# Where the last node's edges are counted: from the graph stage into the recall stage

## The reference

```python
sim = jnp.einsum('bihd,bjhd->bhij', q, k)
sim = jnp.where(causal, sim, neg)
attn = jax.nn.softmax(sim, axis=-1)
out = jnp.einsum('bhij,bjhd->bhid', attn, v)
return out.transpose(0, 2, 1, 3).reshape(b, n, HEADS * DIM) @ Wo
```

```python
src = jnp.concatenate([edge_index[0], loops])
dst = jnp.concatenate([edge_index[1], loops])
e = jax.nn.leaky_relu(a_src[src] + a_dst[dst], negative_slope=0.2)
e_max = jax.ops.segment_max(e, dst, num_segments=M)
ee = jnp.exp(e - e_max[dst])
denom = jax.ops.segment_sum(ee, dst, num_segments=M)
alpha = ee / (denom[dst] + 1e-16)
msg = h[src] * alpha[:, :, None]
agg = jax.ops.segment_sum(msg, dst, num_segments=M)...
```

## Time and profile before

| | |
|---|---|
| median of 3 runs | 5757.28 us (5738.8, 5757.28, 5758.62) |
| the profiled execution | 5745.75 us, its span 5744.1 us |
| mean granted clock of TensorE | 0.846 of full speed |
| TensorE busy | 4668.1 us, 81% |
| VectorE busy | 3530.2 us, 61% |
| ScalarE busy | 2180.4 us, 38% |
| GpSimd busy | 948.0 us, 17% |

### The profile page before, as it was taken

One profiled execution on the slowest core, in us unless ns is written; L12 is line 12 of the kernel. 1 busy time (PEld: TensorE's weight loads), 2 busy tenths in 40 slices (PEclk: granted clock), 3 DMA queues, 4 the chain that ended last, 5 costly groups with the idle time before them and its releaser, 6 DMA issues. The chain is left out here.

```text
span 5744.1 us, 71347 instructions
## 1 busy us (share of the span) xinstructions
PE 4668.1 (81%) x24568; PEld 2826.2 (49%) x24568; DVE 3530.2 (61%) x8762; ACT 2180.4 (38%) x3699; POOL 948.0 (17%) x1055
## 2 busy tenths in 40 slices
PE   7884999999999999999988888884149999963334
PEld 3451444444444444445544444442149988962222
DVE  7547777777777777675525555543125577567655
ACT  1342444444444444444434444442014433420001
POOL 0122111111111111110000000001730000006861
PEclk9555999999999999999978788785579999975556
DMA  1004446555546456655434011001000000000110
GB/s 66 8 3 73 124 131 131 120 131 129 138 112 150 117 129 135 125 132 136 116 115 114 23 34 34 23 1 34 8 7 11 11 15 6 7 9 7 19 13 12
DMA packets 324633, 389.07 MB, mean 68 GB/s; under 512 B 119857, under 2 KB 274749, under 8 KB 323492
## 3 DMA queue, kind: packets, MB, share of 16 engines
q1 hardware_dynamic: 233848, 185.45, 15.8%
q0 software_dynamic: 58368, 172.46, 10.1%
q10 hardware_dynamic: 32076, 26.80, 2.6%
HBM read 313.90 MB, written 70.64 MB: 67 GB/s over the span
## 5 line engine op out<-in xcount | busy, mean ns | idle before, releaser
L1056 PE MATMUL mem_kv<-mem_weights,mem_table 128*128 128x456 f32 x4608 | 1955.7, 546 | 0.0
L1292 DVE SCALAR_TENSOR_TENSOR mem_weights<-mem_above,mem_exps 128x912 f32<-128x912 f32 x1152 | 1273.0, 1105 | 671.8 <-ACT mem_exps L1172 668.8
L1172 ACT ACTIVATE mem_exps<-mem_above 128x912 f32<-128x912 f32 x1152 | 1069.7, 929 | 918.4 <-PE mem_above L1043 918.1
L1056 PEld LDWEIGHTS mem_kv<-mem_weights,mem_table 128*128 128x128 f32 x4608 | 871.2, 189 | 566.9 <-issue 450.9
L2134 DVE TENSOR_REDUCE mha_chunk_max<-mha_max_scores 114x1 f32<-114x342 f32 x864 | 438.5, 513 | 519.5 <-PE mha_max_scores L2002 301.1
L1043 PE MATMUL mem_above<-mem_operands,mem_selector 123*128 123x456 bf16 x2304 | 636.7, 357 | 44.2 <-DVE mem_weights L1292 25.1
L2025 PE MATMUL mha_sums<-mha_probs,mha_value_wide 114*72 114x114 f32 (+1 forms) x5184 | 613.9, 263 | 14.2 <-ACT mha_probs L2116 13.4
L2025 PEld LDWEIGHTS mha_sums<-mha_probs,mha_value_wide 114*72 114x72 f32 (+1 forms) x5184 | 565.8, 145 | 23.7 <-issue 21.3
L2116 ACT ACTIVATE mha_probs<-mha_scores 114x912 f32<-114x912 f32 x324 | 297.6, 930 | 573.2 <-PE mha_scores L2014 371.4
L1043 PEld LDWEIGHTS mem_above<-mem_operands,mem_selector 123*128 123x128 bf16 x2304 | 218.4, 98 | 561.7 <-issue 449.5
L2002 PE MATMUL mha_max_scores<-mha_keys,mha_q 72*114 72x342 bf16 x864 | 277.0, 322 | 225.5 <-issue 172.1
(11 more groups left out here) (590 smaller groups left out, 5521.5 us busy)
## 6 DMA issues: line engine op xcount, KB each, us to landing
mem_table<-in_L_ffn_tables_dram POOLq DMA_DIRECT2D x288, 512.0 KB
mem_operands<-scratch_second_scores SPq DMA_DIRECT2D x216, 256.5 KB
mem_operands<-scratch_first_scores SPq DMA_DIRECT2D x288, 128.2 KB
mem_inv_z<-scratch_inv_z SPq DMA_DIRECT2D x72, 228.0 KB
scratch_second_scores<-mem_sel_parts ACTq DMA_DIRECT2D x81, 171.0 KB
scratch_first_scores<-mem_sel_parts ACTq DMA_DIRECT2D x108, 114.0 KB
scratch_mem_keys<-mem_kvT SPq DMA_DIRECT2D x72, 114.0 KB, 9.8
scratch_mem_values<-mem_value SPq DMA_DIRECT2D x72, 114.0 KB
```

Source lines behind the costliest of these rows:

```text
L1056: last = nc.tensor.matmul(acc[k][:, 0:SPAN], table[:, k, ch, :], W[:, J % 3, c, :], start=(ch == 0), stop=(ch == CHUNKS - 1))
L1172: nc.scalar.activation(E[:, J % 2, :, :], psD[J % 2][:, :, 0:SPAN], ACT.Exp).then_inc(exped, 1)
L1292: nc.vector.scalar_tensor_tensor(W[:, J % 3, :, :], psD[J % 2][:, :, 0:SPAN], 0.0, E[:, J % 2, :, :], ALU.is_ge, ALU.mult).then_inc(weight ...
```

## The change

The count moves into the recall stage. SP loads the two id arrays there, behind the edge keys and ahead of the first queries and keys. GpSimd prepares the row of numbers that the one-hots are compared with (`iota_r`) and clears `hflat`. VectorE makes the one-hots of burst `n` at the end of its steps 0, 2, 3, 5, 6, 8, 14 and 16 of each pair, into four buffers. TensorE does the eight products behind `attend` of steps 1, 3, 4, 6, 7, 9, 15 and 16: eight bursts a pair, 128 in all. They go to 130 more columns of `psO`; ScalarE's copy of each group's output to `oT` takes these along (472 columns in the place of 342), and GpSimd adds them to `hflat`, once a group, 48 times. The copy waits until the add of the group before the last is done with its buffer. At the stage's end VectorE copies the sums to `hsum` and SP stores them to `edge.hist`. The graph stage loads them at its start; its one-hots, its products, `ps_h`, and the store and load at its end are gone. `late_sums`, which stood between two groups' products on TensorE, waits for the number of its rounds (`n_done`) itself.

```diff
-        oT = s.sb("outT", [128, 2, HALF])
+        oT = s.sb("outT", [128, 2, HALF + 2 * LOW])
...
+        hids, lids = s.sb("hist_high", [128, ECOLS], BF16), s.sb("hist_low", [128, ECOLS], BF16)
+        oh_r = s.sb("hist_onehot_high", [128, 4, SELCOL // 2, HIGH * 2], BF16)
+        oh_t = s.sb("hist_onehot_low", [128, 4, SELCOL // 2, LOW * 2], BF16)
+        hsum, hflat = s.sb("hist_pairs", [128, 2, LOW]), s.sb("hist_sums", [128, 2 * LOW])
+        iota = s.sb("iota", [128, LOW])
+        iota_r = s.sb("iota_rows", [128, LOW, 2], BF16)
+        h_in, h_init, hot, h_used, h_added, h_out, h_st = (
+            s.sem(n) for n in ("hist_in", "hist_init", "hot", "hot_used", "hist_added", "hist_out", "hist_stored"))
+        COUNTS = ECOLS // SELCOL
+        HOT_AT, COUNT_AT = (0, 2, 3, 5, 6, 8, 14, 16), (1, 3, 4, 6, 7, 9, 15, 16)
...
             sp.dma_start(edge.late[:, 0:ECOLS], edge.key).then_inc(key_in, 16)
+            sp.dma_start(hids[:, :], edge.hist_high).then_inc(h_in, 16)
+            sp.dma_start(lids[:, :], edge.hist_low).then_inc(h_in, 16)
...
+            sp.wait_ge(h_out, 1)
+            for k in range(2):
+                sp.dma_start(edge.hist[k].rearrange("(p l) -> p l", p=HIGH), hsum[k:128:2, k, :]).then_inc(h_st, 16)
+            sp.wait_ge(h_st, 32)
...
+            nc.gpsimd.iota(iota[:, :], pattern=[[1, LOW]], base=0, channel_multiplier=0,
+                           allow_small_or_imprecise_dtypes=True).then_inc(h_init, 1)
+            nc.gpsimd.memset(hflat[:, :], 0.0).then_inc(h_init, 1)
+            pool.wait_ge(h_init, 2)
+            nc.gpsimd.tensor_copy(iota_r[:, :, :], bc_free(iota[:, :], 128, 2)).then_inc(h_init, 1)
+            pool.wait_ge(h_init, 3)
...
+            for n in range(PAIRS * 3):
+                pool.wait_ge(o_cp, n + 1)
+                past(pool, h_added, n)
+                nc.gpsimd.tensor_tensor(hflat[:, :], hflat[:, :], oT[:, n % 2, HALF:HALF + 2 * LOW], ALU.add).then_inc(h_added, 1)
...
+            def count(n):
+                pe.wait_ge(hot, n * 2 + 2)
+                for j in range(SELCOL // 2):
+                    last = nc.tensor.matmul(psO[:, HALF:HALF + 2 * LOW], oh_r[:, n % 4, j, :], oh_t[:, n % 4, j, :], start=False, stop=False)
+                last.then_inc(h_used, 1)
...
+            pe.wait_ge(h_init, 3)
             for step in range(FIRST_STEP, LAST_STEP):
                 now, ago = flip_of(step), flip_of(step - 1)
                 if now is not None:
                     flip(step, *now)
                 if ago is not None:
                     attend(step - 1, *ago)
+                    if (step - 1) % NF in COUNT_AT:
+                        count((step - 1) // NF * len(COUNT_AT) + COUNT_AT.index((step - 1) % NF))
...
                     past(act, y_mm, 2 * (n - 1))
-                    nc.scalar.activation(oT[:, n % 2, :], psO[:, 0:HALF], ACT.Copy).then_inc(o_cp, 1)
+                    past(act, h_added, n - 1)
+                    nc.scalar.activation(oT[:, n % 2, :], psO[:, 0:HALF + 2 * LOW], ACT.Copy).then_inc(o_cp, 1)
...
+            def one_hots(n):
+                past(dve, h_used, n - 3)
+                for out_, ids, w in ((oh_r, hids, HIGH), (oh_t, lids, LOW)):
+                    nc.vector.tensor_tensor(out_[:, n % 4, :, :].rearrange("p a (t b) -> p a t b", b=2),
+                                            ids[:, n * SELCOL:(n + 1) * SELCOL].rearrange("p (a b) -> p a b", b=2).unsqueeze(2)
+                                            .to_broadcast([128, SELCOL // 2, w, 2]),
+                                            iota_r[:, 0:w, :].unsqueeze(1).to_broadcast([128, SELCOL // 2, w, 2]),
+                                            ALU.is_equal).then_inc(hot, 1)
...
             dve.wait_ge(key_in, 16)
+            dve.wait_ge(h_in, 32)
+            dve.wait_ge(h_init, 3)
...
+                    if step % NF in HOT_AT:
+                        one_hots(p * len(HOT_AT) + HOT_AT.index(step % NF))
...
+            dve.wait_ge(h_added, PAIRS * 3)
+            nc.vector.tensor_copy(hsum[:, :, :], hflat[:, :].rearrange("p (t b) -> p b t", b=2)).then_inc(h_out, 1)
...
-            sp.dma_start(hp[:, :], edge.hist_high).then_inc(e_in, 16)
-            sp.dma_start(hu[:, :], edge.hist_low).then_inc(e_in, 16)
+            sp.dma_start(hboth[:, :, :], edge.hist[:, 0:NODES].rearrange("k (p u) -> p k u", p=TP)).then_inc(h_in, 16)
...
             sp.wait_ge(r_st, NGROUPS * 16)
-            sp.wait_ge(h_out, 1)
-            for k in range(2):
-                sp.dma_start(histD[k].rearrange("(p l) -> p l", p=HIGH),
-                             hsum[k:128:2, k, :]).then_inc(h_st, 16)
-            sp.wait_ge(h_st, 32)
-            sp.dma_start(hboth[:, :, :], histD[:, 0:NODES].rearrange("k (p u) -> p k u", p=TP)).then_inc(h_in, 16)
...
-            def count_last(k):
-                with pe.Fori(k * PER_GROUP, (k + 1) * PER_GROUP) as i:
-                    for m in range(2):
-                        pe.wait_ge(hot, i * 4 + 2 * m + 2)
-                        for j in range(SELCOL // 2):
-                            last = nc.tensor.matmul(ps_h[:, 0:2 * LOW], oh_r[:, m, j, :], oh_t[:, m, j, :], start=False, stop=False)
-                        last.then_inc(h_used, 1)
...
             def late_sums():
+                pe.wait_ge(n_done, 3)
...
-            for k in range(NGROUPS):
-                count_last(k)
-                if k == LATE_AFTER + 1:
-                    late_sums()
-            nc.tensor.matmul(ps_h[:, 0:2 * LOW], zb[:, 0:128], zb[:, 0:2 * LOW], start=False, stop=True).then_inc(h_done, 1)
+            late_sums()
...
-            def count_last(k):
-                with dve.Fori(k * PER_GROUP, (k + 1) * PER_GROUP) as i:
-                    for m in range(2):
-                        dve.wait_ge(h_used, i * 2 + m - 1 if m else i * 2)
-                        cc = bass.ds((i * 2 + m) * SELCOL, SELCOL)
-                        for out_, ids, w in ((oh_r, hp, HIGH), (oh_t, hu, LOW)):
-                            V.tensor_tensor(out_[:, m, :, :].rearrange("p a (t b) -> p a t b", b=2),
-                                            ids[:, cc].rearrange("p (a b) -> p a b", b=2).unsqueeze(2)
-                                            .to_broadcast([128, SELCOL // 2, w, 2]),
-                                            iota_r[:, 0:w, :].unsqueeze(1).to_broadcast([128, SELCOL // 2, w, 2]),
-                                            ALU.is_equal).then_inc(hot, 1)
...
             lookup(0)
-            dve.wait_ge(e_in, 32)
-            count_last(0)
             for k in range(NGROUPS):
                 runs(k)
                 if k == 1:
...
                     table_maxima()
                 if k + 1 < NGROUPS:
                     lookup(k + 1)
-                if k < NGROUPS - 2:
-                    count_last(k + 1)
-                if k == NGROUPS - 1:
-                    count_last(k)
                 if k == LATE_AFTER:
                     late_messages()
             st.settle()
             st = Steps(dve, fstep)
             dve.wait_ge(last_in, 16)
-            dve.wait_ge(h_done, 1)
-            V.tensor_copy(hsum[:, :, :], ps_h[:, 0:2 * LOW].rearrange("p (t b) -> p b t", b=2)).then_inc(h_out, 1)
```

25 lines of the change are left out of this document (7 added, 18 removed).

## The result

| | before | changed |
|---|---|---|
| median of 4 runs | 5751.0 us (5738.8 to 5758.6) | 5644.3 us (5638.1 to 5664.0) |
| ratio | | 0.9823, 95% interval 0.9801 to 0.9844 |
| profiled execution's span | 5744.1 us | 5636.4 us |
| recall stage, first to last instruction | 973.8 us | 933.6 us |
| graph stage, likewise | 502.4 us | 446.9 us |

The kernel is 1.8% faster. A second set of runs, with the kernel before run again beside it, gave 0.9843 (0.9822 to 0.9863).

A forecast was written before the change was run, and what follows sets the result against it. TensorE was taken to bound the recall stage and GpSimd the graph stage. Graph -55, recall +47 and clock -25 gave -33 us, a forecast of 5716 us in a range of 5662 to 5762.

The forecast's parts named there:

- Graph stage: GpSimd's gathers set its end; removing 250 us of VectorE work was to save 57 us, taken as 55.
- (a): Graph stage, gather groups 0 and 1: the first gate was to come 12 us sooner.
- (b): Graph stage, groups 2 to 7: 144 gathers and their lookups were to take 173.3 us busy for 199.2, saving 26 us.
- (c): Graph stage, second gate: GpSimd's wait of 14.76 us was to go, saving 15 us.
- (d): Graph stage, 36 closing gathers: 40.3 us busy for 44.1, saving 4 us.
- no 16 and 15 us gates: Graph stage sign: GpSimd's waits of 16.23 and 14.76 us at two gates were to be absent.
- The bursts: Count products on TensorE in the recall stage: 2.55 us a pair, 41 us over 16 pairs, bounds 30 to 66.
- Loads and store: Recall stage: 3 us for loading the ids before the first keys, about 3 us for the closing copy and store.
- 0.4 us to spare: Recall stage, VectorE's copy of step 5's flip: one-hots delay it but stay hidden, cost 0; otherwise 0.5 us a pair.
- The clock: TensorE's granted clock in the recall stage: recovers sooner in some pairs, gain taken as 25 us.
- Rival 2: Recall stage: dense bursts split the wait, slow stretch shortened in all pairs or missing in many; 5660 us and below; chance 0.13.
- 130 us for a clock that never falls: Recall stage: if the clock never fell, 18.5 busy us would take about 10.3, saving 8 us in each of 16 pairs.

The follow-up runs named there:

- the graph part alone: Changed kernel with the count's loads, one-hots, bursts and adds taken out of the recall stage; ratio 0.9909 to the kernel before, graph stage 447.7 us.
- the filled kernels: Products of zeros added in the wait ahead of flip 9: ratio to the kernel before 0.9736 on the changed kernel (five bursts' worth), 0.9794 on the kernel before (56 products).
- the one-hots only: Changed kernel without its bursts, adds and wider copies, its one-hots made but never awaited; fifteen pairs took 836.5 us, 12.9 more than without one-hots.

## Why the prediction was wrong

**Graph stage: right.** The sum was -57, taken as -55; the profile shows -55.5 and the graph part alone -54.7. By its terms: (a) first gate 12 us sooner, measured 98.0 - 85.8 = 12.2; (b) and (c) together 41, measured from the first gate to the last gather of group 7 (5277.84 to 5556.55 in the earlier trace rows, 5213.29 to 5454.00 now) 278.7 - 240.7 = 38.0; (d) 4, measured 44.1 - 40.3 = 3.8. Of its signs, "no 16 and 15 us gates" came half true: the first gate still waits 12.80 us, which the forecast's own term (a) implies. That GpSimd and not VectorE sets this stage's end, so that only a fifth of the 250 us taken from VectorE counts, held.

**The bursts: near.** Forecast 2.55 us a pair, 38 for the fifteen pairs between the maxima. Of the 120 bursts in them 105 took 0.57 us and the 15 of step 9, at half clock, 0.98: 74.6 us. TensorE's idle time fell by 100.6 - 69.8 = 30.8, so they cost 43.8, inside the forecast's bounds (30 to 66 for 16 pairs). Of the single waits, 3.95 shrank by 1.0 and the others by 1.2 together. (At a full clock, 1.9 us a pair, as the filled kernels showed.)

**Loads and store: near.** Forecast 3 + 3; the stage's start up to the first maxima of t=8 is 3.9 us longer (118.8 against 114.9), its part behind the last ones 5.8 (46.6 against 40.8), which also holds the last pair's bursts.

**VectorE: wrong in mechanism, hidden in effect.** The forecast followed the copy that flip 6 waits for and found 0.4 us to spare. It did not follow the add, for which TensorE's projection waits, and which the one-hots of steps 2 and 3 delay until TensorE stands for 0.8 to 1.1 us. The changed kernel shows nothing of it because the bursts of steps 3 and 4, which the forecast charged in full, lie beside it.

**The clock: here the prediction failed.** The step was: "The main wait is still far longer than any other, so I expect that it still pulls the clock down in most pairs, and that it recovers sooner in some. I take 25 us". The first half is true: the clock still falls in every pair. The second was mis-sized: it recovers sooner in all of them, and the recall stage, forecast 22 us longer, is 40 shorter. The fifteen pairs became 49.9 us shorter with 43.8 us of bursts in them, so all else took 93.7 us less, where 25 had been taken. In busy time that is 698.4 - 74.6 = 623.8 us for the work that took 717.5 before. The granted clock says the same by another way: 287 us were at 0.50 and 102 are now. Work takes nearly twice as long there (six transposes 1.39 us, against 0.80 at 1.00), so half of the difference, some 92 us, is what the clock gave back. Rival 2, with 0.13, is what happened: the slow stretch is shortened in all pairs, to 6.8 us where it was 10 to 24, and the time is below 5660. But its reason, that the bursts split the wait, is not: without the bursts of steps 6 and 7 the wait is 3.96 us again and the stretch still 6.8 in all pairs but the first.

The forecast read the short pair as an exception and took half of its gain. It is one of a cycle of six, and it was the hint that the same instructions run at two speeds, so that a small change of the work could move all pairs to a fast pattern or a slow one. This was in none of the forecast's terms. With its own 130 us for a clock that never falls as the bound, the range would have reached down to 5750 - 55 + 47 - 130 = 5612.

The Trainium skill (TensorE: Matmul & The Clock Gate, HAM oscillation) says that waits between bursts throw the clock back and that products kept together hold it up. The filled kernels agree: 0.99 against 0.82 in the kernel before, 1.00 against 0.93 in the changed one. Its section on PE-mode transpose says that the full clock does not engage for transposes; here six transposes took 0.75 to 0.80 us at the full clock and 1.34 to 1.39 at half, so they do run at both. Whether transposes alone would bring the clock up no run here shows.

**What stays open.** Why pairs settle at 51.2 us in six kernels, mostly at 58.0 in one, and come in cycles where no burst is (of six pairs in the kernel before, of four in the graph part, of two with the one-hots only), was not found. That one burst at step 14 moves them to 51.2 and three to 58.0 shows that it is not the amount of work alone, nor the length of the wait ahead of flip 9 (3.96 us in both), nor the burst inside the slow stretch. That it hangs on when in a pair the clock falls would fit, but no run tested it. So it is also not shown that the changed kernel would keep its 51.2 us if something else in it were edited.

## What to carry to other kernels

Before a count or a copy is moved to make a stage shorter, read the granted clock pair by pair. Where one wait in each round halves TensorE's clock for far longer than it lasts, filling that wait with products, even of zeros, may be worth more than the change: here 2.1% alone, and 2.6% with the change. And if the same instructions take 51 us in one round and 55 in the next, treat the stage's length as uncertain by that much whatever is edited, and don't trust an experiment that moved a little work to have priced it.
